# Expert stage of a graph network: expert weights in the gathered row, results scattered to the output's rows

## The reference, cut to what matters

```python
logits = xt @ Wr + br
probs = softmax(logits); top_p, top_idx = top_k(probs, 2)
weights = top_p / top_p.sum(axis=-1, keepdims=True)
xn = (xt - mu) * rsqrt(var + LN_EPS)
xe = xn[None, :, :] * ln_g[:, None, :] + ln_b[:, None, :]
h = gelu(einsum('end,edh->enh', xe, W1) + b1[:, None, :])
y = einsum('enh,ehd->end', h, W2) + b2[:, None, :]
sel = y of the token's two experts
out = (weights[:, :, None] * sel).sum(axis=1)      # and x + out is returned
```

## Time and profile before

| | us |
|---|---|
| median of 3 runs (lowest, highest) | 3527.32 (3520.94, 3531.6) |
| span of the profiled execution | 3473.6 |
| what lies around the span (median less span; the profiled execution's own time is not listed apart) | 53.7 |
| start of the span to the barrier before the expert block | about 2719 |
| expert block, first matmul of a product to the last `ys` | 2731.6 to 3444.7 |
| end, last scatters and copies to the output | 3444.7 to 3473.6 |

### The profile page before, as it was taken

How to read it: one execution, slowest core, us unless ns; L and a number is a source line. 1 busy time by engine, 2 the same in 40 slices (tenths; PEclk the granted TensorE clock), 3 DMA queues, 4 the chain that set the end, 5 groups by cost and what they waited for, 6 DMA issues and landing times. The chain is left out here.

```text
span 3473.6 us, 47355 instructions
## 1 busy us (share of the span) xinstructions
PE 2350.7 (68%) x11708; PEld 1592.8 (46%) x11709; DVE 1527.9 (44%) x4042; ACT 835.8 (24%) x1644; POOL 2057.1 (59%) x2208
## 2 busy tenths in 40 slices
PE   1488898899667564446666555444433699999996
PEld 1255555555334231223333222212111599899896
DVE  7455555555443242144645533333120455555553
ACT  2233333333222120021111000000000244444442
POOL 0364545556666666446666666666665466766764
PEclk6599999999878776557776666655555799999998
DMA  5222222223322332223333333333333433323324
GB/s 166 85 85 66 75 71 77 81 84 90 91 85 82 89 89 79 67 85 93 99 96 99 94 94 94 93 90 97 89 94 100 134 67 65 65 41 67 66 40 104
DMA packets 166676, 297.70 MB, mean 86 GB/s; under 512 B 51015, under 2 KB 110256, under 8 KB 166352
## 3 DMA queue, kind: packets, MB, share of 16 engines
q0 software_dynamic: 100192, 234.80, 25.9%
q1 hardware_dynamic: 41620, 39.61, 3.7%
q10 hardware_dynamic: 24732, 21.86, 2.0%
HBM read 255.39 MB, written 47.14 MB: 87 GB/s over the span
## 5 line engine op out<-in xcount | busy, mean ns | idle before, releaser
L755 POOL DMA_INDIRECT rows<-table,srcT x1568 | 1545.4, 986 | 965.6 <-issue 434.7
L821 PE MATMUL bank<-rows,onehot 128*128 x1952 | 674.1, 487 | 747.2 <-POOLq L743 695.7
L821 PEld LDWEIGHTS bank<-rows,onehot 128*128 x1952 | 217.9, 112 | 1159.1 <-issue 1031.4
L781 DVE SCALAR_TENSOR_TENSOR onehot<-iota_row,tbase,dstT 128x512 f16 x488 | 366.4, 753 | 633.0 <-PE bank L821 265.2
L1916 ACT ACTIVATE hid<-bank,b 128x256 f32<-128x256 f32 x432 | 181.8, 472 | 368.7 <-PE bank L1868 368.7
L1866 PE MATMUL bank<-xe_high,W_high 128*128 128x256 f32 x864 | 251.5, 291 | 27.0 <-DVE xe_low L1945 26.8
L1866 PE MATMUL bank<-W_high,hid_high 128*128 128x256 f32 x864 | 249.9, 289 | 0.0
L1867 PE MATMUL bank<-xe_low,W_high 128*128 128x256 f32 x864 | 249.6, 289 | 0.0
L1868 PE MATMUL bank<-xe_high,W_low 128*128 128x256 f32 x864 | 249.1, 288 | 0.0
L1868 PE MATMUL bank<-W_high,hid_low 128*128 128x256 f32 x864 | 245.0, 284 | 0.0
L1867 PE MATMUL bank<-W_low,hid_high 128*128 128x256 f32 x864 | 245.0, 284 | 0.0
(11 more groups left out here) (349 smaller groups left out, 3928.3 us busy)
## 6 DMA issues: line engine op xcount, KB each, us to landing
rows<-table,srcT POOLq DMA_INDIRECT x1568, 2.8
W<-in_L_ffn_W_dram SPq DMA_DIRECT2D x14, 1024.0 KB
x_res<-in_x_dram SPq DMA_DIRECT2D x1, 6144.0 KB, 23.1
table<-part ACTq DMA_DIRECT2D x11, 512.0 KB, 3.5
normal<-xn ACTq DMA_DIRECT2D x11, 512.0 KB, 3.3
totals<-x_res SPq DMA_DIRECT2D x11, 512.0 KB, 6.8
table<-part SPq DMA_DIRECT2D x6, 512.0 KB, 2.9
table<-part_b SPq DMA_DIRECT2D x6, 512.0 KB, 2.9
```

Source lines behind the costliest of these rows:

```text
L755: nc.gpsimd.indirect_dma_start(out=rows[:, k % (M * U), 0:ROW], out_offset=None, in_=q.table, in_offset=bass.IndirectOffsetOnAxis(srcT[:, ...
L781: last = nc.vector.scalar_tensor_tensor(onehot[:, ds(slot, U), :], iota_row[:, :].unsqueeze(1).to_broadcast([P, U, P]), base, dstT[:, ds(k ...
L821: last = nc.tensor.matmul(acc[:, 0:ROW], hots[:, ds(hot0 + s * P, P)], ring_rows[:, ds(row0 + s * ROW, ROW)], start=False, stop=False, ski ...
```

## The change

The expert weights of a token are now eight more columns of its row in `normal` (`NROW` = 264), computed by VectorE in `dve_e2`; ScalarE writes the row after that, in a new step `act_e3`. The tensors `shares` and `totals` go. The residual is written to the output itself before the expert block, the two scatters of a tile write plain rows to the output and skip those past its end (`bounds_check`), and what must be added to them is fetched by two new gathers `base` (`load_base`), which wait until the scatters of the tile before have landed. VectorE sums base, bias and result. The index copies of a tile move from GpSimd to VectorE. The two halves of the split of an expert's weights on VectorE (now `dve_split_first`, `dve_split_second`) run in the second and the third tile of an expert in place of after the first. The list of tiles is computed before the last one-hot sums are awaited. The final copy to the output goes.

```diff
...
-        normal = nc.dram_tensor("normal", (NPAD, D), F32).ap()
-        totals = nc.dram_tensor("totals", (NPAD + TT, D), F32).ap()
-        shares = nc.dram_tensor("shares", (P * P, 1), F32).ap()
+        normal = nc.dram_tensor("normal", (NPAD, NROW), F32).ap()
...
-        def dve_split(dve, b, e):
+        def dve_split_first(dve, b, e):
 
             dve.wait_ge(X["high_ready"], e * 2 + 1)
             nc.vector.tensor_tensor(W1_low[b][:, :, :], W1[:, :, :], W1_high[b][:, :, :].bitcast(F32),
                                     ALU.subtract).then_inc(X["weights_ready"], 1)
+
+        def dve_split_second(dve, b, e):
...
                 last = nc.scalar.activation(xnT[:, c, 0:n], bank[c][:, 0:n], ACT.Copy)
             last.then_inc(R["xnT_sb"], 1)
+            act.wait_ge(R["lg_ready"], g + 1)
+            nc.scalar.activation(f1["ex"][:, 0:w, :], f1["lg"][:, 0:w, :], ACT.Exp).then_inc(R["ex_ready"], 1)
+
+        def act_e3(act, g, w):
+            act.wait_ge(R["xn_ready"], g + 1)
+            act.wait_ge(R["gates_ready"], g + 1)
             act.dma_start(normal[ds(first_tile(g) * P, w * P), :].rearrange("(t p) d -> p t d", p=P),
                           xn[:, 0:w, :]).then_inc(R["xn_out"], 16)
-            act.wait_ge(R["lg_ready"], g + 1)
...
+            nc.vector.tensor_tensor(gate1, eq[0], m1.unsqueeze(2).to_broadcast([P, w, E1]), ALU.mult)
+            chain.link(nc.vector.tensor_tensor(gate2, eq[1], m2.unsqueeze(2).to_broadcast([P, w, E1]), ALU.mult))
+            nc.vector.tensor_tensor(xn[:, 0:w, D:NROW], gate1, gate2, ALU.add).then_inc(R["gates_ready"], 1)
...
-                sp.dma_start(shares[:, :].rearrange("(p k) o -> p (k o)", p=P),
-                             row_wt[:, :]).then_inc(R["shares_out"], 16)
+                    if t + w < NT:
+                        sp.dma_start(out[t * P:(t + w) * P, :].rearrange("(t p) d -> p t d", p=P),
+                                     x_cols(t, w).rearrange("p (t d) -> p t d", d=D)).then_inc(X["out_begun"], 16)
+                    else:
+                        sp.dma_start(out[t * P:N, :], x_cols(t, w)[0:N - t * P, :]).then_inc(X["out_begun"], 16)
...
                 start.link(nc.vector.tensor_tensor(rows_i, count[0:1, :], region[0:1, :], ALU.subtract))
+                start.link(nc.vector.tensor_scalar(tiles_i, rows_i, float(TT - 1), float(TILES_MIN * TT), ALU.add, ALU.max))
...
+                all_, empty = slice(0, LCOLS - SUB), slice(LCOLS - SUB, LCOLS)
+                nc.vector.memset(to_list[:, empty], NPAD)
+                nc.vector.memset(from_list[:, empty], 0)
+                dve.wait_ge(R["listed"], 2 * NT)
+                nc.vector.tensor_scalar(past_end[:, all_], listed, 0.0, float(NPAD), ALU.is_equal, ALU.mult)
+                start.link(nc.vector.tensor_scalar(from_list[:, all_], listed, 1.0, 0.0, ALU.subtract, ALU.max))
+                nc.vector.tensor_tensor(to_list[:, all_], from_list[:, all_], past_end[:, all_], ALU.add)
...
+        base = sb("base", [P, SUB, D], F32, ffn)
...
-
-        def copied_out(eng, first, last):
-
-            eng.wait_ge(X["all_out"], 1)
-            for r0 in range(first, last, W):
-                r1 = min(r0 + W, last)
-                k = GW if r1 - r0 == W else 1
-                eng.dma_start(out[r0:r1, :].rearrange("(p k) d -> p (k d)", k=k),
-                              totals[r0:r1, :].rearrange("(p k) d -> p (k d)", k=k)).then_inc(X["copied_out"], 16)
...
+        def expert_tiles(eng, body, before_expert=None, beside=(), after_expert=None):
...
+                    for j, step in enumerate(beside):
+                        body(b, e, j, eng.snap(first + j), lambda: step(b, e, pair))
+                    with eng.Fori(len(beside), tiles) as j:
+                        body(b, e, j, eng.snap(first + j), lambda: None)
...
-                    shift.begin(n + 1)
-                    for newer, older in ((to_mid[:, :], to_old), (to_new[:, :], to_mid), (to_list[:, at], to_new)):
-                        shift.link(nc.gpsimd.tensor_copy(older[:, :], newer))
-                        settled(pool)
-
                 def load(n, at):
                     pool.wait_ge(X["xs_turned"], n + CREDIT)
+                    pool.wait_ge(X["share_taken"], n + CREDIT)
...
                         nc.gpsimd.indirect_dma_start(
-                            out=totals, out_offset=bass.IndirectOffsetOnAxis(to_old[:, s:s + 1], axis=0),
-                            in_=ys[:, s, :], in_offset=None, compute_op=ALU.add).then_inc(X["y_out"], 16)
-
-                def load_shares(n, at):
-                    pool.wait_ge(X["b2_known"], n * KNOWN + KNOWN)
-                    settled(pool)
-                    nc.gpsimd.tensor_copy(shares_of[:, :], share_list[:, at]).then_inc(X["rows_known"], 1)
-                    pool.wait_ge(X["rows_known"], n * 2 + 2)
+                            out=out, out_offset=bass.IndirectOffsetOnAxis(to_old[:, s:s + 1], axis=0),
+                            in_=ys[:, s, :], in_offset=None, bounds_check=N - 1, oob_is_err=False).then_inc(X["y_out"], 16)
+
+                def load_base(n):
+
+                    pool.wait_ge(X["rows_kept"], n + 1)
+                    pool.wait_ge(X["y_out"], n * (16 * SUB) + 16 * SUB)
                     settled(pool)
                     for s in range(SUB):
                         nc.gpsimd.indirect_dma_start(
-                            out=share[:, s:s + 1], out_offset=None, in_=shares,
-                            in_offset=bass.IndirectOffsetOnAxis(shares_of[:, s:s + 1], axis=0)).then_inc(X["shares_loaded"], 16)
-
-                def tile(b, e, j, n):
+                            out=base[:, s, :], out_offset=None, in_=out,
+                            in_offset=bass.IndirectOffsetOnAxis(rows_before[:, s:s + 1], axis=0),
+                            bounds_check=N - 1, oob_is_err=False).then_inc(X["base_loaded"], 16)
+
...
-                    shift_to(n, at)
+                    pool.wait_ge(X["out_begun"], 16 * (LAST + 1))
+                    settled(pool)
                     store(n)
-                    load_shares(n, at)
-
-                pool.wait_ge(X["totals_begun"], 16 * (LAST + 2))
-                pool.wait_ge(R["shares_out"], 16)
+                    load_base(n)
...
+                load_base(n)
...
-                copied_out(act, GROUPS // 2 * W, N)
...
-                def results_out(n):
+                def results_out(n, b):
+                    dve.wait_ge(X["base_loaded"], n * (16 * SUB) + 16 * SUB)
+                    dve.wait_ge(X["rows_kept"], n + 1)
+                    for s in range(SUB):
+                        nc.vector.scalar_tensor_tensor(base[:, s, :], b2[b][:, :], share_of_tile[:, s:s + 1], base[:, s, :],
+                                                       ALU.mult, ALU.add).then_inc(X["base_summed"], 1)
+                    dve.wait_ge(X["y_out"], n * (16 * SUB) + 16 * SUB)
+                    nc.vector.tensor_copy(to_old[:, :], to_new[:, :])
                     dve.wait_ge(X["y_ps"], n + 1)
-                    dve.wait_ge(X["y_out"], n * (16 * SUB) + 16 * SUB)
-                    dve.wait_ge(X["b2_known"], n * KNOWN + KNOWN)
+                    dve.wait_ge(X["base_summed"], n * SUB + SUB)
                     for s in range(SUB):
                         nc.vector.scalar_tensor_tensor(ys[:, s, :], bank[5 + s][:, 0:D], share_of_tile[:, s:s + 1],
-                                                       b2_of_tile[:, s, :], ALU.mult, ALU.add).then_inc(X["y_ready"], 1)
-
-                def tile(b, e, j, n):
+                                                       base[:, s, :], ALU.mult, ALU.add).then_inc(X["y_ready"], 1)
...
+                    at = ds(narrow(dve.snap(e * ECOLS + j * SUB), 0, LCOLS - SUB), SUB)
                     dve.wait_ge(X["xs_turned"], CREDIT + n + 1)
+                    dve.wait_ge(X["rows_kept"], n + 1)
+                    settled(dve)
+                    nc.vector.tensor_copy(share[:, :], xs[:, :, ds(e + D, 1)].rearrange("p s a -> p (s a)")).then_inc(X["share_taken"], 1)
...
-                    results_out(n)
+                    step()
+                    results_out(n, 1 - b if isinstance(j, int) and j == 0 else b)
                     dve.wait_ge(X["y_ready"], n * SUB + 2 * SUB)
-                    dve.wait_ge(X["shares_loaded"], n * (16 * SUB) + 16 * SUB)
-                    for s in range(SUB):
-                        nc.vector.tensor_scalar(b2_of_tile[:, s, :], b2[b][:, :], share[:, s:s + 1], None,
-                                                ALU.mult).then_inc(X["b2_known"], 1)
-                    nc.vector.tensor_copy(share_of_tile[:, :], share[:, :]).then_inc(X["b2_known"], 1)
+                    dve.wait_ge(X["share_taken"], CREDIT + n + 1)
+                    settled(dve)
+                    nc.vector.tensor_copy(to_new[:, :], to_list[:, at])
+                    nc.vector.tensor_copy(share_of_tile[:, :], share[:, :])
```

(10 more changed lines are left out.)

123 lines of the change are left out of this document (39 added, 84 removed).

## The result

| | before | after |
|---|---|---|
| median, run beside each other (lowest, highest), us | 3524.13 (3517.68, 3531.6) | 3482.8 (3479.69, 3497.05) |
| span of the profiled execution, us | 3473.6 | 3481.9 |

The ratio is 0.9894, with a 95% interval of 0.9867 to 0.9922: faster, by 28 to 47 us of 3524. The time lies in the range (3423 to 3483), but at its very edge, and the gain is about half of the forecast.

What follows compares the result with a forecast made beforehand. TensorE's pace was taken as the bound, plus losses at expert changes and a nearly full GpSimd; -12.1 - 39.6 - 24.1 - 4.1 = -79.9 gave a span of 3393.7, with 53.7 around it 3447.4 us, range 3423 to 3483.

Steps and rivals of the forecast that it cites:

- The split: At the seven changes of expert: moving the weight split cuts the loss per change from 8.2 to 2.5 us, -39.6.
- the 57.1 us: Expert stage: time lost beyond TensorE's pace at the seven changes of expert, of 72.2 us lost in all.
- about hold: After a change of expert: the 4 us between `load` landing and its use absorb `base` landing 3 to 5 us late.
- TensorE waiting 5 us or more for `xs` in an expert's third or fourth tile: Expert stage: one of the signs named in advance that would show the forecast wrong.
- GpSimd's tile: Expert stage: GpSimd's work per tile falls from 11.96 to 10.9 us, under TensorE's pace; -12.1 us.
- 54 x 11.82: Expert stage: TensorE's own pace over 54 tile periods, 638.3 us of the 710.5 from first to last `ys`.
- The end: From the last `ys` to the program's end: 5.7 us in place of 29.8, as the output copy goes; -24.1.
- Ahead of the stage: Between the last one-hot sum and the expert stage: less list work on VectorE, -3.1, and GpSimd's preparations gone, -1.0.
- The second: Rival, target DMAs: the bounds test makes each cost 2.0 us, the tile 14.5, total 3571 us; chance 0.07.
- The third: Rival, changes of expert: the weight burst hits the longer chain, 8 us a change stay, total 3487 us; chance 0.07.
- The first: Rival, expert stage: GpSimd stays the bound with a tile of 12.6 us, stage 684, total 3473 us; chance 0.20.
- 53.7 around it: Outside the profiled span: a fixed 53.7 us, added to the forecast span of 3393.7 to give 3447.4.

Runs made afterwards that it cites:

- b1: Kernel before with only the split moved: its halves stand behind `xe_low` of an expert's second and third tile; ratio 1.0011 to the kernel before.
- a0: Changed kernel, unchanged, run and profiled again on a faster chip; 3429.7 us, ratio 0.9856 to the kernel before.
- a10: Changed kernel, unchanged, run once more as the measure for a8 and a9; 3429.9 us, ratio 0.9869 to the kernel before.
- a1: Changed kernel with both halves of the weight split put back behind an expert's first tile; 3429.74 us.
- a9: Changed kernel with raw weights in eight chained pieces and two 128-byte pads that place odd experts' weights like even ones'; 3422.7 us, ratio 0.9857 to the kernel before.
- a8: a9 with both halves of the weight split back behind the first tile; 3430.4 us, ratio 0.9875 to the kernel before.
- b5: Kernel before with the split moved and the raw weights in eight chained pieces; ratio 1.0011 to the kernel before.
- b4: Kernel before with the raw weights in eight chained pieces, split still after the first tile; ratio 0.9988 to the kernel before.
- b6: Kernel before with the split moved and plain scatters for adding ones, sums left out; 3505.9 us on a slower chip, ratio 0.9905 to the kernel before.
- a3: Changed kernel whose reload of raw weights in the expert loop moves only 8 columns of one block; 3407.5 us, ratio 0.9804 to the kernel before.
- b0: Kernel before, unchanged, run and profiled again; ratio 1.0001, median 3477 to 3478 us.
- b3: Kernel before without the final copy of the totals to the output; 3463.1 us, ratio 0.9956 to the kernel before.
- a2: Changed kernel with every operand of TensorE's expert products back at its old on-chip address; 3443.7 us, ratio 0.9901 to the kernel before.
- b2: Kernel before with an unused 192-byte piece ahead of `xe`, shifting `xe`, `hid` and their parts; 3471.5 us, ratio 0.9990 to the kernel before.
- a4: Changed kernel with an expert's raw weights loaded in eight chained pieces of 256 KB; 3423.9 us, ratio 0.9852 to the kernel before.

## Where the prediction failed, and where it held

**The split: the step that failed.** "I take 2.5 us a change in place of 8.2 ... -39.6" measured 0 in the kernel before (b1), about -6 in the changed kernel (a0, a10 against a1) and -12 with paced weights (a9 against a8). The wait for `xe_low` went as forecast, but two readings under the term were wrong.

First, the 57.1 us were where TensorE's time was spent, not what cost it. "GpSimd is nearly full: its tile runs ... 11.96 us" took one tile, the shortest of 54, for all. Its mean of 13.0 is over TensorE's 11.82, and GpSimd waited 8.8 us for others in the whole stage: it set the pace. So a stall of TensorE that went came back as a wait for `xs` (b1, b5: no gain, nor from b4's pacing), and a shorter tile of GpSimd gave what no moved stall had given (b6: -28 of the stage against b1).

Second, the burst of raw weights now comes a tile later, on scatter, landing, `base` and `load` in a row. The 4 us that should "about hold" it faced a landing wait of 7.9. Without the reload the stage is 30 us shorter (a3). "TensorE waiting 5 us or more for `xs` in an expert's third or fourth tile" was the sign of that, and it came.

**GpSimd's tile: prices right, tile too short.** The scatter cost 1.02 us, at the bottom of 0.97 to 1.61, `base` 1.05 for 1.0, the landing 2.0 to 2.35 for 2.1, and a short tile is 10.0 to 10.4 for 10.9. The mean is 11.6 to 11.8, since issues stretch beside VectorE's passes (a gather 2.95 in place of 0.99) and landings beside the burst. "So GpSimd falls under TensorE's pace" did not come true, then. And yet this part is worth more than the -12.1 written, as its tile fell from 13.0. The stage lost 29.7 us (mean of b0 and b3 against mean of a0 and a10); after split (-6) and places (-8), -16 are left. This remainder isn't measured alone, and the parts don't simply add: the split is worth 0, 6 or 12 us by what else is in the way.

**TensorE's pace: a term that was missing.** "54 x 11.82 ... beyond TensorE's own pace" took 11.82 for fixed, since TensorE showed no gap. It rests on where the operands lie; -8 us of the stage (a2). That this helped was luck: the buffers had moved for other reasons.

**The end: -15 to -16 for -24.1.** The copy went as forecast. Not seen was that the program ends some 8 us after its last scatter, which the earlier trace rows can't show, as the copy lay over it (b3).

**Ahead of the stage: -2.6 to -3.6 for -4.1.** This was right. The gather stages, costed at nothing, end perhaps 4 us later (means 2696.6 of nine runs and 2693.0 of six, which overlap); whether the wider rows do it stays open.

**The rivals.** The second is refuted: the bounds test is in the 1.02 us. The third ("the burst of weights hits the longer chain", 0.07) comes closest, and its 3487 is near the measured 3482.8, but in part by luck: what the end and the gather stages took more was offset by the places and by GpSimd's tile. Nor was the longer chain all of it, since in b1 the split bought nothing with the old chain. The first ("GpSimd stays the bound", 0.20) is wrong in its prices and its stage of 684, as GpSimd had rest of 49 us in 673 (a0), but with a tile of 11.6 to 11.8 it was nearer to the truth than the forecast's 10.9.

**The sum.** -79.9 became -30 in the stage, -16, -3.6 and +4, together -46, beside -47 and -44 by the medians on the faster chips and -41 on the first. The wrong "53.7 around it" changed no term: it only tied the span of one chip to the time of another.

## What to carry to other kernels

To find what bounds a stage, add up over the whole stage what each engine waits for on the others: one that hardly waits sets the pace, even where another shows stretches without a gap. One tile, the shortest above all, is no measure for it. Before pricing a stall, ask which engine would fill the time if it went. Look also for the transfer that is triggered by the instruction you move: it comes later by as much, and lands on whatever waits then. A program's end that a copy covers has a floor of its own, so bound a removed tail by what it hides. Take the time of a profiled execution and the medians for one chip only if the numbers say so. A matmul pace without gaps isn't a constant of the kernel: moving buffers moves it.

## What the hardware showed that I had not expected

- The same matmuls start every 0.118 or 0.113 us by where weights and moving data lie: quiet tiles of 11.8 and 11.3 us, both ways in a2 and b2. The cause is open.
- Chips differ: 3474 to 3477 us on three and 3541 on one (seen once) for the same kernel, in the gather stages.
- A plain scatter is issued in 1.00 us (b6), or 1.02 with a bounds test, the adding one in 1.6. A gather issued beside a 128x2048 `W_low` on VectorE took 2.95 (after) in place of 0.99.
- Beside 2 MB of weights at 407 GB/s GpSimd waited 7.9 us for a scatter to land in place of 2.0 to 2.35; with the weights in eight chained pieces no landing wait was over 3.7 (a4).
